# Causal attention on one core: the ten transpositions of a head in one row, the third chunk in another PSUM bank

## The reference

```python
H, KV, HD, HID = (32, 8, 128, 512)
q = (x @ wq).reshape(B, T, H, HD).transpose(0, 2, 1, 3)
k = (x @ wk).reshape(B, T, KV, HD).transpose(0, 2, 1, 3)
v = (x @ wv).reshape(B, T, KV, HD).transpose(0, 2, 1, 3)
q = q * cos + _rotate_half(q) * sin
k = k * cos + _rotate_half(k) * sin
scores = jnp.einsum('bhtd,bhsd->bhts', q, jnp.repeat(k, 4, 1)) * (1.0 / np.sqrt(HD))
scores = jnp.where(jnp.tril(jnp.ones((T, T), dtype=bool)), scores, -jnp.inf)
att = jax.nn.softmax(scores, axis=-1)
out = jnp.einsum('bhts,bhsd->bhtd', att, jnp.repeat(v, 4, 1))
return out.transpose(0, 2, 1, 3).reshape(B, T, H * HD) @ wo
```

## Time and profile before

| | |
|---|---|
| median of 3 runs | 2153.53 us (2153.09 to 2155.36) |
| profiled execution | 2155.01 us, span 2153.0 us |
| mean granted clock of PE | 0.956 of full |
| PE busy | 1975.6 us (92%) |
| DVE busy | 1486.2 us (69%) |
| ACT busy | 1066.2 us (50%) |
| POOL busy | 1042.8 us (48%) |

### The profile page before, as it was taken

How to read it: one execution, slowest core, us unless ns; L and a number is a source line. 1 busy time by engine, 2 the same in 40 slices (tenths; PEclk the granted TensorE clock), 3 DMA queues, 4 the chain that set the end, 5 groups by cost and what they waited for, 6 DMA issues and landing times. The chain is left out here.

```text
span 2153.0 us, 33365 instructions
## 1 busy us (share of the span) xinstructions
PE 1975.6 (92%) x11441; PEld 1604.2 (75%) x11441; DVE 1486.2 (69%) x3684; ACT 1066.2 (50%) x2418; POOL 1042.8 (48%) x801
## 2 busy tenths in 40 slices
PE   4899999999999996897948999999999999988797
PEld 3788888888888874475527888888888888745664
DVE  4666676776767666966776767676766666779286
ACT  3555555565555552434225555656556565533232
POOL 3555564655656431554046555655555565427241
PEclk7999999999999997898969999999999999988899
DMA  5010101011010234136321101010110100041561
GB/s 173 20 30 20 30 20 30 21 30 50 21 30 20 79 109 140 62 103 131 87 88 50 30 13 38 20 30 21 30 50 21 30 20 1 30 142 40 120 122 40
DMA packets 132007, 115.30 MB, mean 54 GB/s; under 512 B 43201, under 2 KB 93441, under 8 KB 131841
## 3 DMA queue, kind: packets, MB, share of 16 engines
q1 hardware_dynamic: 124784, 105.51, 17.0%
q10 hardware_dynamic: 7056, 7.68, 1.3%
HBM read 92.15 MB, written 16.81 MB: 51 GB/s over the span
## 5 line engine op out<-in xcount | busy, mean ns | idle before, releaser
L879 ACT ACTIVATE gqa_prob<-gqa_prob,gqa_nmax 128x256 f32<-128x256 f32 (+3 forms) x512 | 284.1, 556 | 154.8 <-DVE gqa_nmax L993 146.5
L889 ACT CAST gqa_pth<-gqa_pT 128x384 fp32r<-128x384 f32 (+1 forms) x384 | 185.6, 519 | 183.3 <-PE gqa_pT L728 180.8
L993 DVE CUSTOM_DVE_ANT_0 gqa_prob<-gqa_pS,consts 128x256 f32<-128x256 f32 (+3 forms) x512 | 222.6, 486 | 58.7 <-PE gqa_pS L690 56.7
L1162 POOL TENSOR_TENSOR x<-x,consts 128x512 f32<-128x512 f32 x80 | 107.2, 1340 | 303.0 <-ACT x L863 303.0
L1162 POOL TENSOR_TENSOR y<-y,consts 128x512 f32<-128x512 f32 x80 | 107.3, 1341 | 291.9 <-ACT y L863 291.8
L1001 DVE TENSOR_TENSOR gqa_ptl<-gqa_pT,gqa_pth 128x384 fp32r<-128x384 f32 (+1 forms) x384 | 216.9, 593 | 17.8 <-ACT gqa_pth L889 17.8
L728 PE MATMUL gqa_pT<-consts,gqa_prob 128*128 128x128 f32 x1280 | 184.3, 275 | 21.6 <-DVE gqa_ptl L1001 20.1
L668 PE MATMUL gqa_pj<-first_hh,wqh 128*128 128x512 f32 x496 | 196.0, 395 | 0.0
L668 PE MATMUL gqa_pj<-first_hh,wql 128*128 128x512 f32 x496 | 194.9, 393 | 0.0
L668 PE MATMUL gqa_pj<-first_hl,wqh 128*128 128x512 f32 x496 | 194.0, 391 | 0.0
L728 PEld LDWEIGHTS gqa_pT<-consts,gqa_prob 128*128 128x128 f32 x1280 | 154.4, 141 | 49.8 <-DVE gqa_prob L1017 15.8
(11 more groups left out here) (353 smaller groups left out, 5466.2 us busy)
## 6 DMA issues: line engine op xcount, KB each, us to landing
raw_o<-in_wo SPq DMA_DIRECT2D x16, 1024.0 KB, 5.2
raw_q<-in_wq SPq DMA_DIRECT2D x14, 1024.0 KB, 5.5
raw_q<-in_wmod SPq DMA_DIRECT2D x10, 1024.0 KB, 5.2
raw_kv<-in_wkv SPq DMA_DIRECT2D x14, 512.0 KB, 6.8
vp<-mid_hf SPq DMA_DIRECT2D x64, 64.0 KB, 1.8
kp<-mid_hf SPq DMA_DIRECT2D x16, 256.0 KB, 2.3
qp<-mid_hf SPq DMA_DIRECT2D x16, 256.0 KB, 2.5
tail_bd<-vp SPq DMA_DIRECT2D x64, 64.0 KB, 3.2
```

Source lines behind the costliest of these rows:

```text
L879: ins = nc.scalar.activation(p, p, ACT.Exp, scale=-1.0, bias=nmax[r][:, i:i + 1], accum_out=den[r][:, i:i + 1])
L889: nc.scalar.copy(pth[:, n % 2, c:c + w], pT[k % 2][:, 0:w]).then_inc(pt_hi, 1)
L993: nc.vector.tensor_tensor_reduce(prob[r][:, P_OFF[i]:P_OFF[i] + w], pS[s][:, c:c + w], held.mask[:, T - w:T], -1.0, LARGEST, ALU.add, ALU.min,
L1162: nc.gpsimd.tensor_tensor(rot[r % 2][:], rot[r % 2][:], held.sinT, ALU.mult).then_inc(sined, 1)
```

## The change

The ten transpositions of a head stand in one row, and chunk 2 goes into `pO` in place of `pT[0]`. In key steps chunk 2 stays where it was, after the scores, but also goes into `pO`. ACT's `pt_his` and DVE's `pt_los` of chunk 2 move with it: in steps without a key projection they now stand right behind those of chunk 1, ahead of `exps(n + 1)` and `maxes(n + 1)`.

The waits change with the bank. Chunks 0 and 1 wait for their own bank's last subtraction, a step back. Chunk 2 waits until `pO` is free: in an odd step for the addition of tile 1 of the output projection of the pair before, in an even step for the low part of the early output of the pair before. `weigh_early` and tile 1 of `out_proj`, which write into `pO`, now wait for the subtraction of chunk 2 of their own step.

```diff
+        turned = (pT[0], pT[1], pO)
@@ turn
-                        if 3 * n + k >= 2:
-
-                            pe.wait_ge(pt_lo, (3 * n, 3 * n - 1, 3 * n + 1)[k])
+                        if k < 2 and n:
+                            pe.wait_ge(pt_lo, 3 * n - 2 + k)
+                        elif k == 2 and n < 2:
+                            pe.wait_ge(cosed, 2)
+                        elif k == 2 and n % 2:
+                            pe.wait_ge(w_added, TT * (n // 2 - 1) + 2)
+                        elif k == 2:
+                            pe.wait_ge(o_lo, n - 1)
...
-                                mm = pe.transpose(pT[k % 2][:, c:c + P],
+                                mm = pe.transpose(turned[k][:, c:c + P],
@@ weigh_early
                         pe.wait_ge(w_added, TT * (p - 1) + 2)
+                    pe.wait_ge(pt_lo, 3 * (2 * p + 2))
                     pe.wait_ge(v_lo, 2 * p // R0 + 1)
@@ out_proj
+                    if i == 1 and d < NTILES - TT:
+                        pe.wait_ge(pt_lo, 3 * (2 * pair + 3))
@@ the steps on PE
-                    turn(n, ((0, (0,)), (1, (1,))))
+                    turn(n, ((0, (0,)), (1, (1,))) + (() if key_step(n) else ((2, (2, 3)),)))
...
                     for e in step_e(n, 0):
                         project(e)
-                    if not key_step(n):
-                        turn(n, ((2, (2, 3)),))
@@ the steps on ACT, and on DVE with pt_los
-                    pt_his(n, (0, 1))
+                    pt_his(n, (0, 1) if key_step(n) else (0, 1, 2))
...
-                    if not key_step(n):
-                        pt_his(n, (2,))
@@ pt_his, and pt_los alike
-                        nc.scalar.copy(pth[:, n % 2, c:c + w], pT[k % 2][:, 0:w]).then_inc(pt_hi, 1)
+                        nc.scalar.copy(pth[:, n % 2, c:c + w], turned[k][:, 0:w]).then_inc(pt_hi, 1)
```

More of the change, by code:

```diff
@@ L1000, in pt_los @@
                         c, w = PT_CHUNK[k]
-                        nc.vector.tensor_tensor(ptl[:, n % 2, c:c + w], pT[k % 2][:, 0:w], pth[:, n % 2, c:c + w].bitcast(F32),
+                        nc.vector.tensor_tensor(ptl[:, n % 2, c:c + w], turned[k][:, 0:w], pth[:, n % 2, c:c + w].bitcast(F32),
                                                 ALU.subtract).then_inc(pt_lo, 1)
@@ L1103, in _ @@
                             leave(e)
-                    pt_los(n, (0, 1))
+                    pt_los(n, (0, 1) if key_step(n) else (0, 1, 2))
                     for e in step_e(n, 1):
@@ L1120, in _ @@
                         leave(e)
-                    if not key_step(n):
-                        pt_los(n, (2,))
                     if n == NH - 1:
```

## The result

The changed kernel takes 2264.58 us (median of 4 runs, 2261.63 to 2268.16) against 2154.45 for the kernel before: ratio 1.051, 95% interval 1.0498 to 1.0523. The direction was forecast, the size was not: 2228 us, at most 2246. The profiled span grew from 2153.0 to 2263.2 us.

A forecast was written before the change was run, and what follows sets the result against it. The prediction took PE, 92% busy, as the bound. Its terms, 73.6 - 0.6 + 0.5 + 0.3 + 1.1 = 74.9 us, added to 2153.53 gave 2228 us, with a range of 2218 to 2246.

The forecast's parts named there:

- PE is the bound and gives nothing back: Attention stage: PE is almost never idle, so any new wait is added to the time in full.
- The wait of the early block: In 28 key steps `weigh_early` waits for DVE's subtraction of chunk 2: 2.63 us each, 73.6 us in all.
- the sign of being right that was named: List of waits: PE's line 739 waits on `pO` some 30 times, 70 us or more, each near 2.4 us idle.
- One row of ten: Some 64 steps without key or value projection lose a block boundary between transpositions: 0.01 us each, 0.6 us gained.
- Chunk 2 waiting in odd steps: Chunk 2 waits for tile 1's addition: 0.5 us, plus 0.3 once; as a rival 10 us more, chance 0.06.
- DVE's order: Maxima and exponentials come behind one more subtraction, `normed` up to 0.54 us later; nothing late, step 1 within 0.5 us.
- The 1.1 us for the last steps: In the last step of each half the early block waits for one more subtraction: 2 x 0.54 = 1.1 us.
- Transpositions and the clock: Attention stage: rows of ten transpositions last 1.1 us and leave the clock at full, so no cost.
- the rival: Longer rows of transpositions bring half clock in each of 100 steps: 170 us more, 2398 us, chance 0.01.
- The clock falls in the new pauses: Rival: half clock after key steps' pauses; 12 us more if 7 fall, 47 if all 28; chance 0.13.
- eleven stretches: The high end of the range, 2246 us, allowed for eleven half-clock stretches after the new pauses.
- The price of one fall: A 3.4 us stretch at about half clock after a pause loses 1.7 us.

The follow-up runs named there:

- the kernel with its own bank: The changed kernel, but in key steps chunk 2 goes back into `pT[0]` and the early block does not wait for it: 2153.14 us, ratio 0.9985.
- the change with the early subtraction: The changed kernel with ACT's copy and DVE's subtraction of chunk 2 in key steps moved ahead of `exps` and `maxes`: 2151.67 us, ratio 0.9980.
- the run with two pauses: The changed kernel with one unread matmul in the middle of the early block's wait in key steps, splitting PE's pause: 2244.05 us, ratio 1.0413.

## Why the prediction was wrong

- *PE is the bound and gives nothing back*: right. Every wait that was added showed in the time in full.
- *The wait of the early block*: right in place and size. Forecast 2.63 us, measured 2.66; 73.6 against 28 x 2.66 = 74.5. The list has 30 waits ahead of the block with 77.5 us, the sign of being right that was named. With the clock kept up by filling work the changed kernel takes 2225.39, against the forecast 2228.
- *One row of ten*: 0.6 us forecast, 3.3 measured. The boundary was read over one stretch of 0.56 us, in rows rounded to 0.01; the steps show 0.04 to 0.05 where a block goes, and 0.01 in the steps whose chunk 2 already stood beside the values' transpositions. (By the list of steps there are 35 such steps a half, not 32, which changes the forecast by less than 0.1.)
- *Chunk 2 waiting in odd steps* and *DVE's order*: nothing measurable in the steps between, as forecast; chunk 2 waits for the addition twice, 0.5 us in all. The 1.1 us for the last steps did not show: from step 58 to the end of the stage the first half took 0.6 us less than before, the second 0.1 more.
- *Transpositions and the clock*: rows of ten leave it at full (1.00 in both windows of the kernel with its own bank), so the rival did not come. The rule of the Trainium skill ("TensorE: Matmul & The Clock Gate", Part 4: PE-mode transpose), that transpositions do not count as busy like other matmuls, is neither refuted nor shown by this: a row of ten lasts 1.1 us, and even a pause of 1.7 us left the clock at full here.
- **The step that failed: "The clock falls in the new pauses", priced at 0.13 and kept to eleven stretches by the range.** The argument against it was that "dense matmuls stand on both sides of the new ones". They do, and the clock fell after 25 of 28 all the same. The row that spoke for it (a pause of 2.53 us, then 0.51 of the clock) was the nearest to the 2.47 us of the new wait; the row against it, 1.40 us, was farther. The price of one fall was right: 1.7 us forecast, 1.57 measured, 39 us in all. With 25 falls the sum would have been 2228 + 25 x 1.57 = 2267; measured 2264.58.

The version that the runs point to, the change with the early subtraction, beats both: 0.9980 of before (0.9971 to 0.9989), 4 us. The one with its own bank is as good within the intervals.

## What to carry to other kernels

When a bank is lent to a second tenant, its next writer inherits the wait for the last reader; look on that reader's engine for what stands in front of it, here a reciprocal and four scalings that wait for exponentials. On an engine without slack, count a new pause twice: its length, and the clock behind it, read from the pauses in the trace that are nearest in length; dense matmuls beside them are no reason to leave it out, and short pauses close together count too. And a transposition or a tile that seems to lie anywhere may be covering the emptying of a bank.

## What the runs showed of the hardware that was not expected

The falls recur. In the changed kernel 3.4 us at half clock start at 131.3, 182.5, 233.7 us and so on, 51.2 us apart, while a group of four steps with a fall lasts 51.1 us and one without 49.5. So the fall begins a little later behind the block's start each time: 0.56 us in step 5 of the first half, 1.46 in step 45, and step 49, the next, is spared. In the kernel before with the one wait added, a group lasts 51.17 us, the fall drifts only from 0.40 us in step 5 to 0.71 in step 49, and step 49 falls too. This fits a key step that falls bringing the next one to almost the same point of that rhythm, until the small difference has added up; no run tests it. In the run with two pauses, eight falls came in the first half and four in the second. Which key steps fall was not settled by more than this.
